# A graph network's adjacency built in steps of one edge chunk instead of two, with one-hots on POOL

## The reference

```python
q, k, v = linear(x, wq, bq), linear(x, wk, bk), linear(x, wv, bv)
scores = jnp.sum(q[dst] * k[src], axis=-1) * scale + (edge_weight[:, None] @ we + be)[:, 0]
exp_s = jnp.exp(scores - segment_max(scores, dst)[dst])
attn = exp_s / jnp.maximum(segment_sum(exp_s, dst)[dst], 1e-12)
out = segment_sum(v[src] * attn[:, None], dst)
x = layer_norm(x + out + linear(x, ws, bs), g1, b1)
x = layer_norm(x + ffn(x), g2, b2)
...
idx = jnp.argmax(xf @ router_w.T + router_b, axis=-1)   # 32 experts, one per node
x = x + relu(relu(xf @ W1[idx] + b1[idx]) @ W2[idx] + b2[idx])
```

## Time and profile before

| | |
|---|---|
| median of 3 runs | 1892.36 us (1878.16 to 1903.58) |
| profiled execution | span 1885.6 us, 41069 instructions; no time outside of the span is given for it |
| TensorE busy | 1656.9 us (88%) |
| VectorE busy | 1193.9 us (63%) |
| ScalarE busy | 965.5 us (51%) |
| POOL busy | 300.8 us (16%) |
| adjacency stage, first product to last sum | 159.5 to 888.0 us |
| attention stage | 888.1 to about 1484 us |

### The profile page before, as it was taken

How to read it: one execution, slowest core, us unless ns; L and a number is a source line. 1 busy time by engine, 2 the same in 40 slices (tenths; PEclk the granted TensorE clock), 3 DMA queues, 4 the chain that set the end, 5 groups by cost and what they waited for, 6 DMA issues and landing times.

```text
span 1885.6 us, 41069 instructions
## 1 busy us (share of the span) xinstructions
PE 1656.9 (88%) x11015; PEld 1378.6 (73%) x11015; DVE 1193.9 (63%) x3327; ACT 965.5 (51%) x2962; POOL 300.8 (16%) x397
## 2 busy tenths in 40 slices
PE   2898999999799999999899999999999789419960
PEld 1796888888688888887688888888888779315640
DVE  3927898988688889898555555555555578701111
ACT  1566888888588888887233333333333345103210
POOL 0022000000000000000111111111110067375435
PEclk9999999999899999999999999999999889656555
DMA  6054333333433333334822222222210100047634
GB/s 159 28 129 115 104 105 104 106 103 105 140 104 104 106 105 103 104 105 112 164 76 77 76 76 76 76 78 75 76 75 37 53 17 0 6 117 214 181 113 121
DMA packets 226999, 180.40 MB, mean 96 GB/s; under 512 B 41884, under 2 KB 218038, under 8 KB 223544
## 3 DMA queue, kind: packets, MB, share of 16 engines
q1 hardware_dynamic: 189327, 112.46, 21.6%
q0 software_dynamic: 21408, 61.20, 9.7%
q10 hardware_dynamic: 16224, 6.27, 1.5%
HBM read 84.94 MB, written 99.11 MB: 98 GB/s over the span
## 4 chain that ended last, share of the span: by engine, by line
PE 78%; DVE 6%; DMA 5%; POOL 4%; issue 3%; SPq 2%; ACT 1%; POOLq 0%; DVEq 0%; ACTq 0%
PE bank L1371 29%; PE bank L1404 15%; PE bank L1392 11%; PE bank L1356 9%; PE bank L1411 3%; PE bank L1486 3%; PE bank L1493 2%; PE bank L1478 2%; PE bank L1444 2%; PE bank L1436 2%; POOL arena L691 2%; POOL xs_dram L669 2%; SPq L458 1%; DMA V<-in_x 1%; DMA arena<-in_x 1%
## 5 line engine op out<-in xcount | busy, mean ns | idle before, releaser
L784 ACT ACTIVATE arena<-bank,tables 128x128 f32<-128x128 f32 x2048 | 585.2, 369 | 144.5 <-PE bank L1356 144.4
L1371 PE MATMUL bank<-arena 128*125 128x128 f32 x4096 | 585.9, 286 | 11.8 <-DVE arena L1055 11.8
L1371 PEld LDWEIGHTS bank<-arena 128*125 128x125 f32 x4096 | 488.4, 188 | 65.1 <-DVE arena L1055 11.9
L1055 DVE TENSOR_TENSOR arena<-iota_row,tables 128x250 f32<-128x250 f32 x1024 | 421.1, 412 | 0.1
L1081 DVE SCALAR_TENSOR_TENSOR arena<-arena,tables,bank 125x128 f32<-125x128 f32 x1023 | 351.9, 344 | 86.5 <-PE bank L1371 37.1
L1404 PE MATMUL bank<-V,arena 125*125 125x256 f32 x1250 | 296.4, 382 | 5.6 <-ACT arena L810 5.6
L810 ACT COPY arena<-bank 125x500 f32<-125x500 f32 (+1 forms) x175 | 90.8, 533 | 379.5 <-PE bank L1411 379.5
L1404 PEld LDWEIGHTS bank<-V,arena 125*125 125x125 f32 x1250 | 223.3, 188 | 38.0 <-ACT arena L810 10.3
L1122 DVE CUSTOM_DVE_ANT_0 arena<-arena 125x3200 f32<-125x3200 f32 x25 | 87.3, 3493 | 222.2 <-ACT arena L793 222.2
L622 POOL COPY gidx<-arow 125x1 uint32 (+1 forms) x25 | 36.4, 1455 | 1182.2 <-DVE wk_sb L1122 856.7
L1356 PE MATMUL bank<-dist_rhs,arena 5*128 5x128 bf16 x2048 | 201.6, 218 | 4.2 <-DVE tables L1039 3.4
(11 more groups left out here) (219 smaller groups left out, 1665.5 us busy)
## 6 DMA issues: line engine op xcount, KB each, us to landing
adj<-arena SPq DMA_DIRECT2D x512, 125.0 KB
xs_dram<-zeros SPq DMA_DIRECT2D x64, 112.0 KB, 3.2
V<-xs_dram SPq DMA_DIRECT2D x56, 128.0 KB, 2.3
ys_dram<-arena SPq DMA_DIRECT2D x56, 128.0 KB, 1.9
w_dram<-in_L_ffn_W SPq DMA_DIRECT2D x2, 2048.0 KB
V<-in_x SPq DMA_DIRECT2D x5, 625.0 KB
q_dram<-arena ACTq DMA_DIRECT2D x25, 125.0 KB, 2.3
wq_sb<-q_dram SPq DMA_DIRECT2D x25, 125.0 KB, 7.8
```

Of the source, the lines that this page charges most:

```text
L784: ins = nc.scalar.activation(Ys[:, q, k, :], bank[2 + s][:, k * LO:(k + 1) * LO], ACT.Relu, scale=nval_tab[:, bass.ds(i, 1)])
L1055: ins = V_.tensor_tensor(Xs[:, s, cols, :], iota_row[:, 0:TILE].unsqueeze(1).to_broadcast([P, SUB, TILE]), code_tab[:, bass.ds(g * GC + k ...
L1371: ins = mm(o, Xs[:, j % STAGES, k, :], Ys[:, j % STAGES, k, :], start=(k % SUB == 0), stop=(k % SUB == SUB - 1))
```

## The change

A step now holds one chunk of 128 edges (`SUB` = 1) instead of two. That makes 1406 steps instead of 1015, and with whole turns 1408 slots in 704 groups and 44 turns, instead of 1024 slots in 512 groups and 32 turns. A group has 2 chunks instead of 4: 1408 distance matmuls, one-hot rows and product matmuls (2816 instructions) instead of 2048 (4096), and 1408 sums instead of 1024. The set-up counts over 784 chunks instead of 392 pairs, for 11 blocks of steps instead of 8, and gathers 11 times instead of 16.

The 3125 sources are now 24 blocks of 131 columns instead of 25 of 125 (padded to 128). So products have 120 partitions of 131 columns, and a row of the adjacency has 3144 numbers instead of 3200. Scores, masks and weights run over 7 blocks of 448 columns instead of six of 512 and one of 128.

The destination one-hots move from VectorE to POOL: one `tensor_scalar` a chunk, 128 by 120, against a column of a copy of the codes (`held`), which POOL makes for 8 groups at a time. POOL's program for the stage stands ahead of its first `fetch`. TensorE's product now waits on `sums_ready` as well.

```diff
-SUB = 2
+SUB = 1
-LO = 128
-ROW = NT * LO
+HI, LO = 24, 131
+ROW = HI * LO
+MW = WIN * HI
+KB = 448
+NCOL = 7 * KB
-SCH = [(c, min(512, ROW - c)) for c in range(0, ROW, 512)]
+SCH = [(c, KB) for c in range(0, NCOL, KB)]
...
@@ block.gpsimd, after the gathers of the edge table @@
+            pool.wait_ge(tab_set, SBLK)
+            pool.wait_ge(terms_stored, 16 * SUB * SBLK)
+
+            def hold_codes(n, h):
+                nc.gpsimd.tensor_copy(held[:, h, :], code_tab[:, bass.ds(n * HELD, HELD)]).then_inc(codes_held, 1)
+
+            hold_codes(0, 0)
+
+            def one_hots(g, j, i):
+                h = j // LOADG
+                if j % LOADG == 0:
+                    pool.wait_ge(codes_held, 2 * i + h + 1)
+                if j % LOADG == 2 and not (isinstance(i, int) and i == TURNS - 1 and h):
+                    wait_from(pool, x_ready, g - 2)
+                    hold_codes(2 * i + h + 1, 1 - h)
+                wait_from(pool, prod_done, g - STAGES + 1)
+                pool.sem_inc(pool_mark, 1)
+                for k in range(GC):
+                    c = j % LOADG * GC + k
+                    ins = nc.gpsimd.tensor_scalar(Xs[:, j % STAGES, k, :], iota_row[:, 0:MW], held[:, h, c:c + 1], None,
+                                                  ALU.is_equal)
+                ins.then_inc(x_ready, 1)
+
+            turns(pool, one_hots)
...
@@ block.vector @@
-            def one_hot(g, s, k):
-                cols = slice(k * SUB, (k + 1) * SUB)
-                ins = V_.tensor_tensor(Xs[:, s, cols, :], iota_row[:, 0:TILE].unsqueeze(1).to_broadcast([P, SUB, TILE]),
-                                       code_tab[:, bass.ds(g * GC + k * SUB, SUB)].unsqueeze(2).to_broadcast([P, SUB, TILE]),
-                                       ALU.is_equal)
-                if k == GROUP - 1:
-                    ins.then_inc(x_ready, 1)
...
-                    prev = stage[0:TILE, q, k - 1, :] if k else stage[0:TILE, (q - 1) % STAGES, GROUP - 1, :]
-                    ps = product_bank(j)[0:TILE, k * LO:(k + 1) * LO]
+                    prev = stage[0:MW, q, k - 1, :] if k else stage[0:MW, (q - 1) % STAGES, GROUP - 1, :]
+                    ps = product_bank(j)[0:MW, k * LO:(k + 1) * LO]
...
-                    if not (isinstance(i, int) and i == TURNS - 1 and j > BODY - STAGES):
-                        one_hot(g + STAGES - 1, (q - 1) % STAGES, k)
...
@@ block.tensor, product @@
                 pe.wait_ge(x_ready, g + 1)
+                wait_from(pe, sums_ready, g - STAGES + 1)
+                wait_from(pe, sums_ready, g - STAGES + 1)
                 for k in range(GC):
-                    o = product_bank(j)[0:TILE, k // SUB * LO:(k // SUB + 1) * LO]
+                    o = product_bank(j)[0:MW, k // SUB * LO:(k // SUB + 1) * LO]
```

More of the change, by code:

```diff
@@ L176, in gnn_moe @@
         assert SBLK * SUB * TABW <= edges_only
-        cmp_o = view(4 * P)
-        s_row, o_row, iota_c = view(4 * P), view(4 * P), view(4 * P)
-        cmp_s, s_row, o_row, iota_c = (v[:, 0:NS] for v in (cmp_o, s_row, o_row, iota_c))
+        cmp_o = view(NS)
+        s_row, o_row, iota_c = view(NS), view(NS), view(NS)
+        cmp_s = cmp_o
         diag_flat = view(SBLK * P)
@@ L202, in gnn_moe @@
         assert at[0] <= edges_end
+        held = view(2 * HELD).rearrange("p (h c) -> p h c", h=2)
         step_end = at[0]
@@ L295, in gnn_moe @@
             "code_set", "idx_set", "rel_set", "tabT_done", "tab_set", "keep_set"))
-        gath_in = [sem(f"gath_in{b}") for b in range(SBLK)]
+        s_copied, codes_held = sem("s_copied"), sem("codes_held")
+        gath_in = [sem(f"gath_in{b}") for b in range(-(-SBLK // 2))]
+        gathered = [16 * min(2, SBLK - 2 * b) for b in range(-(-SBLK // 2))]
         last_set, last_stored, last_in, arow_set = (sem(n) for n in ("last_set", "last_stored", "last_in", "arow_set"))
@@ L486, in _ @@
             for b in range(SBLK):
-                sp.wait_ge(gath_in[b], 16 * SUB)
+                sp.wait_ge(gath_in[b // 2], gathered[b // 2])
                 for u in range(SUB):
@@ L939, in _ @@
             i1 = iota_row[0:1, :]
[L940 to L943, removed]
+            lo_sq, lo_sqh = cmp_o[0:1, 0:LO], cmp_o[0:1, LO:2 * LO]
+            od(V_.tensor_tensor(lo_sq, i1, i1, ALU.mult))
+            rounded(lo_sqh, lo_sq, 1.0 / P, 0.0)
+            od(V_.tensor_scalar_mul(dist_line[:, 0, :], lo_sqh, float(P)))
+            od(V_.scalar_tensor_tensor(dist_line[:, 1, :], lo_sq, -1.0, dist_line[:, 0, :], ALU.add, ALU.subtract))
             od(V_.tensor_copy(dist_line[:, 2, :], i1))
@@ L1023, in _ @@
             for b in range(SBLK):
-                dve.wait_ge(gath_in[b], 16 * SUB)
+                dve.wait_ge(gath_in[b // 2], gathered[b // 2])
                 codes = gath[:, b, :, 0:CHUNK]
@@ L1317, in spread @@
                 pe.wait_ge(diag_set, 1)
-                mm(bank[0][:, 0:NS], ones[0:PP, :], s_diag, start=True, stop=True).then_inc(rows_bc, 1)
+                mm(bank[0][:, 0:512], ones[0:PP, :], s_diag[:, 0:512], start=True, stop=True)
+                mm(bank[1][:, 0:NS - 512], ones[0:PP, :], s_diag[:, 512:NS], start=True, stop=True).then_inc(rows_bc, 1)
                 pe.wait_ge(diag_set, 2)
+                pe.wait_ge(s_copied, 1)
                 mm(bank[1][:, 0:4 * PP], ones[0:PP, :], e_diag, start=True, stop=True).then_inc(rows_bc, 1)
```

80 lines of the change are left out of this document (39 added, 41 removed).

## The result

The changed kernel took 2216.51 us (median of 4 runs, 2209.24 to 2233.30) beside 1895.07 us for the kernel before (4 runs): ratio 1.172, 95% interval 1.165 to 1.179. The forecast of 1875 us had the sign wrong, and the range, up to 2010, did not hold it.

A forecast was written before the change was run, and what follows sets the result against it. TensorE was taken to bound the kernel, in the adjacency stage. Set-up +7, stage -22, attention's start +5 and tiles -7 took 1885.6 to 1869 us; 6.8 for the median gave 1875, range 1800 to 2010.

The forecast's parts named there:

- TensorE's share: Adjacency stage: a group with half the chunks shrinks from 1.40 to 0.72 us of TensorE time.
- TensorE's clock: Rival, adjacency stage: idling TensorE drops its clock, a group takes 1.19 us; low half the time, 1938 us; chance 0.09.
- VectorE's chain: Adjacency stage: dependent sums set the pace, 0.505 us a looped step, 1.01 a group; stage 706 us, 22 less.
- The one-hots on POOL: Adjacency stage: 0.4 us each on POOL, 0.8 a group, costing nothing while two fit in 1.01 us.
- POOL is the pace: Rival, L638 in the adjacency stage: POOL's one-hots set the group from 0.50 us each; at 0.6, 2009 us; chance 0.12.
- SBUF contention: Rival, adjacency stage: sums wait on average half a POOL one-hot, 239 us more, 2114 us; chance 0.05.
- The stores: Adjacency stage: one DMA a group lands in time, costing nothing; upper end 28 us.
- Set-up: Ahead of the adjacency stage: more counting, fewer gathers and a smaller memset, +7 us (2 to 14).
- The attention's start: Between last sum and first mask: gathers now stand behind all one-hots, +5 us (2 to 10).
- Its tiles: Attention's 25 tiles: scores of fewer columns in still 42 matmuls, -7 us (-3 to -10).

The follow-up runs named there:

- split version: Changed kernel with groups of three, one-hots two on POOL, one on VectorE, sum factors at a fixed place; 0.958 with first product twice in first 16 groups.

## Why the prediction was wrong

**TensorE's share** was the step that failed, twice over. First its size: I halved 1.40 us by the chunks and got 0.72. But a group has a part that does not shrink with its chunks; at the higher clock the estimate above is 0.87, at the lower 1.484 is measured. What that part is made of wasn't looked into. Alone it would have cost nothing, since 0.87 is under the 1.01 of the sums. Second, and this is the loss, its clock. The rival *TensorE's clock* had the right place and the right start (rows 4 show the low clock there) and the wrong size: it priced the low group by 0.72 x 1.65 = 1.19 us where it is 1.484, and it argued that "TensorE is at full work again, and on such work it rose in rows 4". The work of rows 4 was eight product matmuls a group; here there were four, and it never rose, though the profile's windows show TensorE busy without a break. The rival had 0.09, half of the stage low, and 1938 us; the whole stage low at 1.484 us is 704 x 1.484 = 1045 us against 1045.9 measured. Of the 340 us over the forecast's 706, the low clock holds some 250: with the clock up POOL's pace would give 704 x 1.131 = 796.

The Trainium skill (TensorE: Matmul & The Clock Gate, section "Why this matters for your kernels") advises keeping TensorE busy without a break to get the higher clock, and leaving no long idle gaps between bursts of matmuls to keep it. No gap of this loop is long: the weight loads, which go ahead of the matmuls, stand 0.20 us before the products and 0.25 before the distances in the timeline above. By that advice alone the clock should have risen; the measurement decides, and it stayed at 0.50 for over 1000 us.

**VectorE's chain**: right. 0.50 us a looped step, the sum 0.352 for 0.35. It just isn't the bound. Its gain of 22 us was not what it seemed, though: the stage before holds the store wait of 17.5 us (the windows' 669 busy of 681 us has it, and I read past it), so most of those 22 us would have come from moving the gathers and not from the sums.

**The one-hots on POOL**: mis-sized. 0.4 us was taken; 0.581 is the duration, and from start to start it is 0.565 (1.131 for two). The rival *POOL is the pace* named 0.6 and 2009 us. It did not come about only because TensorE was slower still; with the clock up it did, and the run took 1971.4 us beside 1907.4.

**SBUF contention**: right to be left out. The sums took 0.352 us under POOL's one-hots and 0.346 before without them. The page SBUF — State Buffer of the Trainium skill (section "Who interferes with whom") said so for an instruction with one SBUF input, and the trace agrees. In the split version VectorE's one-hot has both inputs in SBUF, beside POOL; it took 0.277 to 0.286 us where it took 0.276 with POOL idle, so there too nearly nothing. Why the instruction of rows 8 took 0.95 us stays open. VectorE's one-hots without and with POOL beside them (busy us, mean ns; 340 and 400 us of the loop):

```profile
L1066 DVE TENSOR_TENSOR arena<-iota_row,tables 128x120 f32<-128x120 f32 x458 | 126.3, 276 | 0.0
```
```profile
L1110 DVE TENSOR_TENSOR arena<-iota_row,arena 128x120 f32<-128x120 f32 x293 | 83.8, 286 | 0.0
```

**The stores**: right at nothing; 2.3 us to landing, and no idle time of VectorE is put down to them.

**Set-up**: +6.8 us for +7. **The attention's start**: +8.7 for +5, within 2 to 10. **Its tiles**: +7.5 for -7. The scores' matmuls did get shorter, but they are now broken by a wait, which the chain shows in 18 of the 25 tiles:

```profile
1361.40 4.89 PE bank L1414 x24
1366.29 0.20 issue
...
1366.66 0.10 DVE wk_sb L1132
1366.76 0.04 issue
1366.80 3.92 PE bank L1414 x18
```

4.89 + 3.92 is 8.81 us for 9.03; 0.51 of waiting for VectorE's L1132 to free a bank comes on top, +0.3 a tile. The shorter last block used to come where VectorE needed the time; seven equal ones of 448 columns leave it none. That is argued from the chain, not tried.

**The remaining -18.5 us** lie behind the attention, where the change does nothing. From the experts' first matmul to the last it is 135.7 us before and 121.3 after, 14.4 of the 18.5. The same stretch of that stage, 266 us behind the last scores, before, then after:

```profile
1716.20:1766.20 50.00, 50.00 (x159) 30.70 (x160) 8.46 (x20) 14.65 (x40) 25.48 (x44) 0.50 0.66 192
```
```profile
2056.80:2106.80 50.00, 45.83 (x216) 29.46 (x216) 11.47 (x27) 19.57 (x54) 28.06 (x49) 0.84 0.81 237
```

TensorE had the lower clock for all of it in one execution and mostly the higher in the other. That may also be what spreads the runs of the kernel before over 2%: of its runs in one experiment the shortest, 1874.0 us, has a mean clock of 0.939 and the longest, 1897.8, one of 0.911. What makes the clock differ wasn't tested.

**Why a higher clock alone would not have saved it.** The kernel before spends 728.6 us on the stage; 1408 steps match that at 0.517 us each. With POOL's one-hots and the clock up a step takes 0.565. With VectorE's own it took 0.554, but there TensorE's repeated product sets the pace; VectorE is busy 1.04 us a group, so 0.52 a step would be its best (an estimate), and that only equals the kernel before. The forecast's stage of 706 us would have been 22 us better, 1%; only the split version, at 0.45 a step, gets well below.

## What to carry to other kernels

When a change takes work out of TensorE's groups, don't scale the measured group down: subtract matmuls and keep the fixed part, and do it at both levels of the clock, since the lighter group may never leave the level in which it starts. A stage in which TensorE is busy 100% at a clock of 0.50 is the sign to look for, and the cheapest test is to add work: if the kernel with repeated matmuls is faster, the clock is the cause. Then balance what comes next, here the one-hots over two engines, before paying for a clock that the next engine can't use.

## What the runs showed of the hardware

- The profile's busy share alone did not tell TensorE's clock: at 100% busy it stayed at 0.50 with two products a group, for over 1000 us, and rose within some 20 us with three or four. Two more bf16 matmuls of 5 rows a group did not lift it.
- What lifts it and what holds it differ: in the split version the same groups rose only after some 75 us from a low start, and stayed up at once from a high one, with TensorE idle for 49 of 400 us. Waiting for POOL in groups of three (57 of 80 us busy) it fell again after tens of us.
- After a stop of some 10 us TensorE went on at 0.50. The kernel before, with eight product matmuls a group, was back at 1.00 in 5 us; with six and the one-hots on VectorE it took some 15.
- While the attention's two gathers ran in mid-stage, the sums waited 10.8 to 13.5 us for a group's store, in the kernel before and in both with the one-hots on VectorE. In the changed kernel, without gathers beside them, half of the stores landed within 2.3 us.
- POOL's `tensor_scalar` of 128x120 f32 against one factor a partition takes 0.581 us, 0.565 from start to start; VectorE's comparison of the same size 0.276.
- A VectorE step that reads its factor at a register's address takes 0.50 us from sum to sum, the same with a fixed address 0.38.
